# First weight pieces of softmax attention loaded and split in linear attention's last batch, in the buffers of its key and value weights

## The reference, cut to what matters

```python
x = x + 0.5 * quantised_linear(layernorm(x))
x = x + linear_attention(layernorm(x))      # 16 query heads, 4 key/value heads, head dim 128, elu + 1
x = x + 0.5 * quantised_linear(layernorm(x))
x = x + 0.5 * routed_mlp(layernorm(x))      # the 128 highest of 1024 tokens of a batch, 256 -> 1024 -> 256
x = x + softmax_attention(layernorm(x))     # 16 heads, head dim 128
x = x + 0.5 * routed_mlp(layernorm(x))
```

## Time and profile before

| what | value |
|---|---|
| runs | 3502.99, 3504.67 and 3505.31 us, median 3504.67 |
| the profiled execution | 3506.28 us; its span, first to last instruction, 3504.5 us |
| mean granted clock of TensorE | 0.983 of full speed |
| TensorE matmul, busy | 3339.6 us, 95% |
| VectorE, busy | 2666.2 us, 76% |
| ScalarE, busy | 2044.9 us, 58% |
| GpSimd, busy | 1057.1 us, 30% |
| linear attention hands over to softmax attention | about 718 to 729 us |

### The profile page before, as it was taken

How to read it: one execution, slowest core, us unless ns; L and a number is a source line. 1 busy time by engine, 2 the same in 40 slices (tenths; PEclk the granted TensorE clock), 3 DMA queues, 4 the chain that set the end, 5 groups by cost and what they waited for, 6 DMA issues and landing times.

```text
span 3504.5 us, 52704 instructions
## 1 busy us (share of the span) xinstructions
PE 3339.6 (95%) x19398; PEld 2861.0 (82%) x19398; DVE 2666.2 (76%) x4957; ACT 2044.9 (58%) x3908; POOL 1057.1 (30%) x1274
## 2 busy tenths in 40 slices
PE   3898999989999999999999999999999999999995
PEld 2777878868888888888888888888888888888884
DVE  5788796767876787876788677886778767876776
ACT  3676767646556556556565556555555565556552
POOL 3786656632222112122121221212212131213112
PEclk8999999999999999999999999999999999999997
DMA  2221212110001000001000001000000010001000
GB/s 83 70 85 50 66 55 70 58 37 13 13 19 29 15 13 13 15 23 28 13 14 13 25 19 43 13 13 25 25 14 14 13 34 28 16 19 29 26 19 20
DMA packets 98525, 104.21 MB, mean 30 GB/s; under 512 B 10336, under 2 KB 88800, under 8 KB 98144
## 3 DMA queue, kind: packets, MB, share of 16 engines
q1 hardware_dynamic: 98272, 100.85, 9.7%
HBM read 87.18 MB, written 13.63 MB: 29 GB/s over the span
## 4 chain that ended last, share of the span: by engine, by line
PE 70%; DVE 6%; ACT 3%; DMA 0%; issue 0%; POOL 0%; DVEq 0%; SPq 0%; ACTq 0%; POOLq 0%
PE at_ps_job L1927 12%; PE at_ps_job L35 7%; PE at_ps_job L37 7%; PE at_ps_job L36 6%; PE at_ps_o L35 6%; PE at_ps_o L37 6%; PE at_ps_o L36 6%; PE at_ps_s L35 6%; PE at_ps_s L36 6%; PE at_ps_s L37 6%; DVE at_neg_max L1854 1%; ACT x_resident L1678 1%; DVE at_probT_lo L1721 1%; PE at_ps_job L646 1%; DVE at_oT_lo L1752 0%; DVE ch_r L97 0%
## 5 line engine op out<-in xcount | busy, mean ns | idle before, releaser
L1637 ACT ACTIVATE at_probT_hi<-at_ps_job 128x512 fp32r<-128x512 f32 x1024 | 611.4, 598 | 889.9 <-PE at_ps_job L1927 887.2
L1721 DVE TENSOR_TENSOR at_probT_lo<-at_ps_job,at_probT_hi 128x512 fp32r<-128x512 f32 x1024 | 702.8, 686 | 275.5 <-ACT at_probT_hi L1637 265.1
L1678 ACT ACTIVATE x_resident<-at_ps_s,at_neg_max 128x1024 f32<-128x1024 f32 x512 | 570.7, 1115 | 151.6 <-DVE at_neg_max L1854 146.5
L1854 DVE TENSOR_REDUCE at_neg_max<-at_ps_s 128x1 f32<-128x1024 f32 x512 | 622.2, 1215 | 5.3
L1927 PE MATMUL at_ps_job<-ident,x_resident 128*128 128x128 f32 x4096 | 613.7, 272 | 5.0 <-DVE at_probT_lo L1721 3.4
L1927 PEld LDWEIGHTS at_ps_job<-ident,x_resident 128*128 128x128 f32 x4096 | 495.9, 140 | 97.7 <-issue 7.3
L35 PE MATMUL at_ps_o<-at_probT_hi,at_v_lo 128*128 128x512 f32 x1024 | 446.3, 436 | 8.9 <-DVE at_oT_lo L1752 7.8
L1613 POOL TENSOR_TENSOR at_w_hi<-at_w_raw,ch_cols 128x256 fp32r<-128x256 f32 x192 | 117.6, 613 | 1107.1 <-PE at_ps_job L37 1086.3
L35 PE MATMUL at_ps_s<-at_k_hi,at_q_lo 128*128 128x512 f32 x1024 | 445.1, 435 | 0.0
L37 PE MATMUL at_ps_o<-at_probT_lo,at_v_hi 128*128 128x512 f32 x1024 | 404.6, 395 | 0.0
L36 PE MATMUL at_ps_s<-at_k_hi,at_q_hi 128*128 128x512 f32 x1024 | 402.0, 393 | 0.0
(11 more groups left out here) (347 smaller groups left out, 7480.8 us busy)
## 6 DMA issues: line engine op xcount, KB each, us to landing
at_w_raw<-attn_w SPq DMA_DIRECT2D x256, 128.0 KB, 2.3
at_w_raw<-mlp_w SPq DMA_DIRECT2D x112, 128.0 KB, 2.3
li_wo_hi<-li_wo_kept SPq DMA_DIRECT2D x24, 256.0 KB, 2.7
li_wo_lo<-li_wo_kept SPq DMA_DIRECT2D x24, 256.0 KB, 3.0
li_wq_hi<-li_wq_kept SPq DMA_DIRECT2D x48, 128.0 KB, 2.3
li_wq_lo<-li_wq_kept SPq DMA_DIRECT2D x48, 128.0 KB, 2.8
x_resident<-x SPq DMA_DIRECT2D x4, 1024.0 KB, 13.1
out<-x_resident SPq DMA_DIRECT2D x4, 1024.0 KB, 4.9
```

The costliest lines, as they stand in the source:

```text
L1637: nc.scalar.activation(ph[:, i // TC, 4 * half:4 * half + 4, (i % TC) * P:(i % TC + 1) * P], c.turned_bank(2 * TB * u + 2 * i + half), ACT ...
L1678: nc.scalar.activation(prob[:, slot % 2, :], ps_s[slot % 2][:], ACT.Exp, bias=nmax[:, slot:slot + 1], accum_out=rsum[:, u % 2, slot:slot + ...
L1721: nc.vector.tensor_tensor(pl[at], c.turned_bank(2 * TB * u + 2 * i + half), ph[at].bitcast(F32), ALU.subtract).then_inc(s_pl, 1)
L1854: nc.vector.tensor_reduce(nmax[:, slot:slot + 1], ps_s[slot % 2][:], AX.X, ALU.max, negate=True).then_inc(s_max, 1)
```

## The change

The key and value weights and their bias of linear attention stay allocated to the end. Softmax attention's split weights, its output buffers `oh` and `ol`, and its ring of raw pieces become views of them (`AttentionWeights`), in place of buffers of its own. SyncE loads WK 0, WV 0, WV 1 and WQ 0 in linear attention at step 106, into what was the bias. GpSimd splits them at steps 110, 112, 114 and 116. In softmax attention the list at t = 0 holds WK 1 alone, the counts that GpSimd and TensorE wait for are lower by the pieces done early, and a count of 0 is not waited for. `iota` and `before` become bf16, which holds their values exactly.

```diff
-        self.iota = sb("iota", [P, P], F32)
-        self.before = sb("before", [P, P], F32)
+        self.iota = sb("iota", [P, P], BF16)
+        self.before = sb("before", [P, P], BF16)
...
+class AttentionWeights:
+    def __init__(self, kv):
+        hi, lo = (part[:].rearrange("p a b -> p (a b)") for part in (kv.hi, kv.lo))
+        n = KT * HD
+        self.wh, self.wl = (x[:, 0:3 * n].rearrange("p (a w) -> p a w", a=3) for x in (hi, lo))
+        self.wvh, self.wvl = (x[:, 3 * n:5 * n].rearrange("p (k d) -> p k d", k=KT) for x in (hi, lo))
+        self.out_hi, self.out_low = (x[:, 5 * n:7 * n] for x in (hi, lo))
+        self.raw = [kv.bias[:, i * n:(i + 1) * n] for i in range(RING)]
...
+RING = 4
+EARLY = ((WK, 0), (WV, 0), (WV, 1), (WQ, 0))
+EARLY_LOAD, EARLY_SPLIT = 106, (110, 112, 114, 116)
...
# linear_attention_phase, SyncE, behind the fetch of query weights of step t
+                if t == EARLY_LOAD:
+                    sp.wait_ge(c.taken, by_dve["KV", 2 * B - 1, TB - 1])
+                    for i, (part, v) in enumerate(EARLY):
+                        sp.dma_start(aw.raw[i], a["attn_w"][v, :, part * D:(part + 1) * D]).then_inc(s_early, 16)
...
# linear_attention_phase, GpSimd, ahead of the background of step t
+                if t in EARLY_SPLIT:
+                    i = EARLY_SPLIT.index(t)
+                    part, v = EARLY[i]
+                    hi, lo = aw.parts(part, v)
...
+                    pool.wait_ge(s_early, 16 * len(EARLY))
+                    nc.gpsimd.tensor_tensor(hi, early, none, ALU.add).then_inc(s_early_hi, 1)
+                    pool.wait_ge(s_early_hi, i + 1)
+                    nc.gpsimd.tensor_tensor(lo, early, hi.bitcast(F32), ALU.subtract).then_inc(s_early_lo, 1)
...
# attention_phase
+        def splits(part, v):
+            return v + 1 - sum(piece[0] == part for piece in EARLY)
+        def wait_split(pe, part, v):
+            if splits(part, v) > 0:
+                pe.wait_ge(s_w[part], splits(part, v))
...
-                yield from ((WK, 0), (WV, 0), (WV, 1), (WQ, 0), (WK, 1))
+                yield WK, 1
...
-                            pe.wait_ge(s_w[wpart], v + 1)
+                            wait_split(pe, wpart, v)
...
-                            pe.wait_ge(s_w[WV], 2 * v + 2)
+                            wait_split(pe, WV, 2 * v + 1)
...
-                            pe.wait_ge(s_w[WO], v + 1)
+                            wait_split(pe, WO, v)
```

More of the change, by code:

```diff
@@ L681, with __init__, parts @@
 class KvWeights:
[L684 to L689, removed]
+    def __init__(self, nc, ctx):
+        self.hi = ctx.enter_context(nc.sbuf_tensor("li_wkv_hi", [P, KT, 2 * KVH * HD], F32R))
+        self.lo = ctx.enter_context(nc.sbuf_tensor("li_wkv_lo", [P, KT, 2 * KVH * HD], F32R))
+        self.bias = ctx.enter_context(nc.sbuf_tensor("li_bkv", [P, 2 * KVH * HD], F32))
+class AttentionWeights:
[6 more added lines that the diff above has]
+        self.raw = [kv.bias[:, i * n:(i + 1) * n] for i in range(RING)]
+    def parts(self, part, v):
+        if part == WV:
+            return (w[:, :, (v % 2) * HD:(v % 2 + 1) * HD] for w in (self.wvh, self.wvl))
+        at = min(part, 2)
+        return self.wh[:, at, :], self.wl[:, at, :]
+WK, WQ, WV, WO = range(4)
+RING = 4
+EARLY = ((WK, 0), (WV, 0), (WV, 1), (WQ, 0))
+EARLY_LOAD, EARLY_SPLIT = 106, (110, 112, 114, 116)
 def first_layer_phase(nc, sh, c, kv, a):
@@ L1350 @@
 UNITS = B * H
-RING = 4
 SLOTS = TB * UNITS
@@ L1410, in turns_at, with attention_phase @@
             yield ("TURNED", number), "turn", number + 1
-def attention_phase(nc, sh, c, a, out):
-    WK, WQ, WV, WO = range(4)
+def attention_phase(nc, sh, c, kv, a, out):
     heads = {u: head_jobs(u) for u in range(-1, UNITS + 1)}
@@ L1440, in attention_phase @@
         ph, pl = pair("probT", [P, 2, TB, CH])
-        oh, ol = pair("oT", [P, CH])
+        oh, ol = aw.out_hi, aw.out_low
         nmax = sb("neg_max", [P, TB], F32)
@@ L1602, in split @@
                 if part == WV:
-                    hi, lo = (w[:, :, (v % 2) * HD:(v % 2 + 1) * HD] for w in (wvh, wvl))
+                    hi, lo = aw.parts(part, v)
                     src, none = src.rearrange("p (k d) -> p k d", k=KT), nil3
@@ L1613, in split @@
                 nc.gpsimd.tensor_tensor(hi, src, none, ALU.add).then_inc(s_wh[part], 1)
-                pool.wait_ge(s_wh[part], v + 1)
+                pool.wait_ge(s_wh[part], splits(part, v))
                 nc.gpsimd.tensor_tensor(lo, src, hi.bitcast(F32), ALU.subtract).then_inc(s_w[part], 1)
-                pool.wait_ge(s_w[part], v + 1)
+                pool.wait_ge(s_w[part], splits(part, v))
                 nc.gpsimd.sem_inc(s_split, 1)
@@ L2041, in build @@
         c = Chain(nc, sh, lambda name, shape, dt: ctx.enter_context(nc.sbuf_tensor(f"ch_{name}", shape, dt)))
-        with ExitStack() as linear:
-            kv = KvWeights(nc, sh, linear)
-            first_layer_phase(nc, sh, c, kv, a)
-            linear_attention_phase(nc, sh, c, kv, a)
+        kv = KvWeights(nc, ctx)
+        first_layer_phase(nc, sh, c, kv, a)
+        linear_attention_phase(nc, sh, c, kv, a)
         sh.recycle()
-        attention_phase(nc, sh, c, a, out)
+        attention_phase(nc, sh, c, kv, a, out)
 def kernel(**inputs):
```

21 lines of the change are left out of this document (12 added, 9 removed).

## The result

| | before | after |
|---|---|---|
| median, us | 3504.82 (3502.99 to 3506.01) | 3495.29 (3493.29 to 3496.91) |
| ratio | | 0.9972, 95% interval 0.9965 to 0.9980 |
| the profiled execution, us | 3506.28, span 3504.5 | 3493.63, span 3491.9 |
| mean granted clock | 0.983 | 0.988 |

The change takes 9.5 us off the median. The forecast was 3497.1 us, 7.6 us less than before; rival A, in which the clock stays up over the shorter hole, was 3495.3 us.

A forecast was written before the change was run, and what follows sets the result against it. It took TensorE's stream, busy 95% of the span, to bound the kernel. 6.84 us for the earlier start plus 0.8 for the clock, nothing elsewhere, made 7.6 us less: 3497.1 us from the median 3504.67, range 3494.5 to 3500.5.

The forecast's parts named there:

- rival A: Hand-over: the clock does not fall in the shorter hole; 9.3 us less, 3495.3 us; chance 0.15.
- The start, 6.84 us: Hand-over: TensorE's first softmax matmul needs only the barrier, starting at 721.90 instead of 728.74; 6.84 us removed.
- Rival C: Hand-over: TensorE's new program is not ready at the barrier; 4.9 us lost, 3502.0 us; chance 0.07.
- All four waits: First softmax projections: the diff leaves none of the four waits on early weight pieces; no separate size given.
- WK 1 and the spill: Early softmax attention: the fifth piece keeps 4.6 us of cover and the first exponential finds the spill landed; no cost.
- Linear attention, zero: Steps 106 to 116: four loads fit SyncE's idle time and four split pairs fit GpSimd's gaps; cost nothing.
- D: Linear attention gives some back through late pairs or fetches behind the loads, 0.8 to 2.8 us; 3499.1 us; chance 0.07.
- bf16, zero: VectorE multiplies and comparisons, in the tail and elsewhere: narrowing one operand changes no duration; 0 us.
- E: Tail and batch 0 of linear attention: mixed types cost; if doubled, 3.4 us slower, 3508.1 us; chance 0.04.
- The clock, 0.8 us: Hand-over: the clock still falls, for 3.4 us, losing 1.7 us against 2.5 before; 0.8 us gained.
- The range: Whole kernel: time expected between 3494.5 and 3500.5 us.

The follow-up runs named there:

- e1: Kernel before, with 22 unused matmuls on TensorE between the barrier and the first projection, which still waits for its piece: 3504.32 us, ratio 1.0000.
- e4: Changed kernel with only WK 0 loaded and split early; WV 0, WV 1, WQ 0 and WK 1 at t = 0: 3503.05 us, ratio 0.9992.
- e8: Changed kernel with each early piece split twice on GpSimd, same result: 3496.28 us, one execution.
- e2: Kernel before, with only iota and before made bf16: 3505.30 us, ratio 1.0002.
- e11: Changed kernel unaltered, profiled a third time: 3494.60 us, one execution.
- e5: Changed kernel unaltered, profiled a second time: 3495.04 us, ratio 0.9973.
- e3: Changed kernel with shared buffers and bf16 kept, but no piece early, all five loaded and split at t = 0: 3503.77 us, ratio 0.9998.
- e10: Changed kernel with 4 unused matmuls on TensorE behind linear attention's last matmul, ahead of the barrier: 3494.14 us, ratio 0.9970.
- e9: Changed kernel with only the first K projection job (6 matmuls) moved ahead of the barrier: 3495.55 us, ratio 0.9972.
- e6: Changed kernel with 12 unused matmuls on TensorE behind linear attention's last matmul, ahead of the barrier: 3497.89 us, ratio 0.9980.
- e7: Changed kernel with the first two K projection jobs (12 matmuls) moved ahead of the barrier: 3496.65 us, ratio 0.9977.

## Why the prediction was right, and where it was off

**The start, 6.84 us: right.** TensorE starts 0.04 us behind SyncE's first issue, as taken. B went from 10.07 to 3.26, which is 6.81. *Rival C*, a program not ready at the barrier, is refuted by that row and by e1, where the old program restarts as promptly. The Trainium skill (Runtime: NRT & Kernel Launch, Instruction fetch mechanics) would allow for a fetch at the taken branch; no time for one is seen between SyncE's 719.96 and TensorE's 720.00. A fetch that all engines make together, inside the 1.5 us between GpSimd's last addition and SyncE's first issue, would not be seen so.

**All four waits: right, and needed.** e4 shows that the sum stood on the whole set. The forecast named this in one sentence only, on the diff; the price of the three missing pieces, 7.1 of the 9.1 us, was worth a rival. A cheaper rival of the change itself was not tried either: WK 0 is issued behind the 1 MB spill and lands after 4.92 us, where the median of the 256 loads of this kind is 2.3. What it would give to issue it ahead of the spill stays open.

**WK 1 and the spill: right.** WK 1's split runs from 725.28 to 726.71, waiting for its DMA and not, as forecast, for K 0's second half. It was put at up to 728.7, in an execution that is 1.9 us later at this place, so the end agrees. TensorE takes the piece at 729.86, so the cover is 3.2 us; 4.6 was forecast, and 1.5 of the difference is the clock that stayed up. The spill lands 5.0 us after its issue, at about 725.0, and the first exponential, at 731.32, waits for its row maximum.

**Linear attention, zero: right.** A is 95.28 against 95.36, for the loads and the splits together. The rule of the Trainium skill that was weighed against the change (SBUF — State Buffer, Who interferes with whom) agrees where its condition is met. Of the four hi halves only the first is longer, 0.79 us against 0.63, 0.63 and 0.60, and only there does VectorE run an instruction that reads two SBUF tensors at that moment:

```profile
649.88 0.54 DVE L611 TENSOR_TENSOR ch_r_rounded<-ch_o,ch_r_rounded 128x256 fp32r<-128x256 f32 x1 [1.32 <-ACT ch_r_rounded L459]
```

In e8 the same meeting makes it 0.81 us, and the 1.06 us of the earlier trace rows stand beside such an instruction too (L607 from 605.41 to 606.24). Beside L1307 and L1319, which take an input from PSUM, the halves keep their time. The 0.2 us are covered by the gap. D is refuted, with e8 as the stronger evidence.

**bf16, zero: right**, by the rows and by e2. The 56 instructions of each kind outside the tail have kept their means too (406 and 347 ns in after, 406 and 348 in before). E is refuted.

**The clock, 0.8 us: the term that was mis-sized.** The step held it "to be the less likely" that the clock would stay up in the shorter hole, on the strength of one hole of 3.15 us and one place in the tail where it fell, and gave rival A 0.15. Measured: it stays up in 3 of 4 profiled executions that keep the change's own hole at the hand-over (after, e8 and e11; it falls in e5), and then the term is 9.12 - 6.81 = 2.3 us; when it falls it is 20.85 - 13.27 - 6.81 = 0.8, the forecast's number. Both prices were close (2.5 and 0.8 were given). What was wrong was to take one outcome from one row: the same hole can have either, as e5, and e3 at the other hole, show.

**What the median holds beyond that.** 6.8 and 2.3 are 9.1, and the median moved by 9.5. D, the part after the first scores, has two groups of values as well, 2763.1 to 2763.8 and 2764.9 to 2765.8, in kernels with and without the change, and they go with the clock: after the first scores it was low for 34.6 to 35.0 us in all, nearly all of it in the tail, in the seven executions with the lower value, and for 37.5 to 42.1 us in the six with the higher. Of the five kernels without all early pieces (before to e4) one has the lower value, of the eight with them six. Whether the change favours it or these few executions chanced on it stays open. So does the scatter of some 4 us ahead of the first added instruction, where the same code comes to the fetch of step 106 at anything from 619.87 to 623.91 us; the clock's course in the first 150 us differs between these executions too.

**The range** held the result, since it took in rival A. The forecast of 3497.1 was 1.8 us high, and one fall of the clock at the hand-over is priced at 1.5; how often it fell in the executions that were not profiled is not known. That the median, 3495.29, meets rival A's 3495.3 so closely is luck: the base moved from 3504.67 to 3504.82, A's clock term was 0.2 too large, and the 0.4 us beyond the stretch were not forecast.

## What to carry to other kernels

At a barrier between phases, look at what the next phase's first instructions read: if it can be loaded and prepared in idle time of the phase before, in buffers that are dead by then, the whole wait goes. One piece of four, moved alone, gave 2.0 of 9.1 us here, so look for the next wait behind the one that goes. Work may be put ahead of a barrier until it would arrive later than the last other engine; from there on what is put ahead is handed back. And a hole that costs clock is to be priced as two outcomes with a chance for each, from several executions, for one trace shows one of them.

## What the runs showed of the hardware

- A TensorE hole of 3.26 us has cost either nothing or 1.54 us, in executions of one and the same kernel. Across the kernels here, e10's of 2.34 us had no fall and e9's of 2.02 us had one; the one at step 107, 2.98 to 3.15 us, had one in twelve executions and none in one. The length did not order them.
- Leaving one phase for the next takes some 1.5 us from the end of GpSimd's last instruction to SyncE's first issue, when GpSimd comes last, and 1.71 us from TensorE's last matmul to SyncE's first issue when TensorE does (e6 and e7).
- At full clock the split chain on GpSimd, 1.61 us per piece, was too slow for the first projections of the old kernel (e1); with 5.0 us of them at half clock none of them had waited for it.
- A comparison or a multiply of 128x128 on VectorE takes as long with a bf16 operand beside a float32 one as with both in float32: 281 against 282 ns and 347 against 347.
- A hi half of 128x256 on GpSimd took 0.60 to 0.63 us, and 0.79 to 1.06 us in the four places looked at (after, e6, e8 and before) where VectorE ran an instruction that reads two SBUF tensors at that moment.
